# Two stacked attention layers: the stretch between the layers rebuilt, part of the next images' preparation moved into both layers

## The reference

```
layer 0:  f = x Wf + bf   g = x Wg + bg   (8 columns each)   h = x Wh + bh   (64 columns)
          x1 = gamma0 * softmax(g f^T) h + x
layer 1:  q = x1 Wq + bq  k = x1 Wk + bk  v = x1 Wv + bv      (64 columns each)
          out = gamma1 * softmax(q k^T) v + x1
```

## Time and profile before

| what | value |
|---|---|
| median of three runs | 4473.93 us (4473.06 to 4486.53) |
| the profiled execution: time, span | 4475.64 us, 4473.8 us |
| mean granted clock of TensorE | 0.934 |
| busy share: PE, DVE, ACT, POOL | 95%, 74%, 72%, 41% |
| first transposes; first fg_abs; first maxima (L773) | 11.1, 25.76, 86.75 us |
| first scores of layer 0 of image 0; last | 137.8; some 364 us |
| first scores of layer 1 of image 0 | 422.64 us |
| last product of values of layer 1 of image 0 | 671.63 us |

### The profile page before, as it was taken

How to read it: one execution, slowest core, us unless ns; L and a number is a source line. 1 busy time by engine, 2 the same in 40 slices (tenths; PEclk the granted TensorE clock), 3 DMA queues, 4 the chain that set the end, 5 groups by cost and what they waited for, 6 DMA issues and landing times.

```text
span 4473.8 us, 84431 instructions
## 1 busy us (share of the span) xinstructions
PE 4235.0 (95%) x25704; PEld 1535.0 (34%) x25704; DVE 3322.0 (74%) x6409; ACT 3205.1 (72%) x5810; POOL 1826.6 (41%) x845
## 2 busy tenths in 40 slices
PE   5998999989999899999999999999999989999899
PEld 3224332243322533234322433224332243322433
DVE  4776887768777687767877678776887768877687
ACT  1575986659766697657977579775896758967598
POOL 1693008910099001980039600496005940079200
PEclk6897999979999799998999889998999989999799
DMA  0000000000000000000000000000000010000000
GB/s 29 1 11 20 1 1 10 11 20 1 11 1 11 20 1 10 1 11 20 1 11 1 20 10 1 10 1 26 4 1 11 1 29 1 1 11 11 19 1 10
DMA packets 13604, 41.64 MB, mean 9 GB/s; under 512 B 2620, under 2 KB 2620, under 8 KB 10812
## 3 DMA queue, kind: packets, MB, share of 16 engines
q1 hardware_dynamic: 13244, 36.78, 2.7%
HBM read 19.99 MB, written 8.39 MB: 6 GB/s over the span
## 4 chain that ended last, share of the span: by engine, by line
PE 80%; issue 11%; DVE 5%; ACT 3%; POOL 1%; SPq 0%; DVEq 0%; POOLq 0%; DMA 0%; ACTq 0%
PE sum_banks L521 20%; PE score_banks L509 20%; PE sum_banks L430 18%; PE score_banks L410 9%; PE sum_banks L452 3%; PE score_banks L585 3%; PE score_banks L359 2%; PE sum_banks L382 2%; DVE tile_max L773 1%; PE score_banks L344 1%; ACT e_whole L705 1%; POOL e_sum L311 1%; DVE x_abs L882 1%; ACT g_tr L627 1%; ACT f_tr L672 1%
## 5 line engine op out<-in xcount | busy, mean ns | idle before, releaser
L705 ACT ACTIVATE e_whole<-score_banks,exp_bias,down 128x512 f32<-128x512 f32 x2048 | 1574.6, 774 | 215.2 <-DVE o_tr L934 170.4
L311 POOL TENSOR_TENSOR e_sum<-e_sum,e_whole 128x1024 f32<-128x1024 f32 x704 | 1659.5, 2357 | 83.5 <-ACT e_whole L645 32.4
L773 DVE TENSOR_REDUCE tile_max<-sum_banks 128x1 f32<-128x512 f32 (+1 forms) x2128 | 1363.8, 685 | 424.7 <-PE sum_banks L382 421.4
L645 ACT ACTIVATE e_whole<-score_banks,no_bias,down 128x1024 f32<-128x1024 f32 x1024 | 1228.5, 1204 | 546.3 <-PE score_banks L410 536.7
L934 DVE TENSOR_SCALAR_CACHE_REDUCE o_tr<-score_banks,neg_down 128x1024 f32<-128x1024 f32 x1024 | 1314.4, 1284 | 315.7 <-PE score_banks L509 265.9
L430 PE MATMUL sum_banks<-e_whole,proj 128*64 128x512 f32 x4096 | 1119.1, 626 | 0.0
L521 PE MATMUL sum_banks<-e_whole,v_scaled 128*64 128x512 f32 x4096 | 1058.9, 598 | 28.2 <-DVE v_scaled L924 8.4
L308 POOL TENSOR_TENSOR e_sum<-e_whole 128x1024 f32<-128x1024 f32 x32 | 75.5, 2358 | 1930.2 <-ACT e_whole L645 1930.2
L509 PE MATMUL score_banks<-k_high,q_split 128*64 128x512 f16 x4096 | 810.8, 388 | 36.3 <-ACT e_whole L705 18.1
L509 PE MATMUL score_banks<-k_low,q_split 128*64 128x512 f16 x4096 | 803.1, 384 | 0.0
L382 PE MATMUL sum_banks<-f_tr,g_tr 33*128 33x512 f16 x2128 | 695.5, 400 | 21.7 <-DVE tile_max L773 18.6
(11 more groups left out here) (111 smaller groups left out, 2093.9 us busy)
## 6 DMA issues: line engine op xcount, KB each, us to landing
x_in<-in_x_dram SPq DMA_DIRECT2D x19, 1024.0 KB, 4.8
out_dram<-x_mid SPq DMA_DIRECT2D x32, 256.0 KB, 2.7
k_high<-k_high SPq DMA_DIRECT2D x32, 128.0 KB, 2.2
k_low<-k_low SPq DMA_DIRECT2D x32, 128.0 KB, 2.2
gammas<-in_L_conv_gamma_dram SPq DMA_DIRECT2D x2, 0.5 KB
w<-in_L_conv_wg_dram SPq DMA_DIRECT2D x1, 2.0 KB
w<-in_L_conv_bg_dram SPq DMA_DIRECT2D x1, 0.0 KB
w<-in_L_conv_wf_dram SPq DMA_DIRECT2D x1, 2.0 KB
```

Source lines behind the costliest of these rows:

```text
L311: nc.gpsimd.tensor_tensor(acc, acc, e_whole[:, i % U0, :], ALU.add).then_inc(e_added, 1)
L645: nc.scalar.activation(e_whole[:, i % U0, :].rearrange("p (a n) -> p a n", a=2), score_banks[:, 2 * (i % 2):2 * (i % 2) + 2, :], ACT.Exp, ...
L705: nc.scalar.activation(e_whole[:, u, h * BANK:(h + 1) * BANK], score_banks[:, 2 * (u % 2) + h, :], ACT.Exp, bias=exp_bias[:, u:u + 1], sca ...
L773: nc.vector.reduce_max(tile_max[:, blk, j:j + 1], sum_banks[:, (2 + j % banks) % 4, :], AX_X).then_inc(a_used, 1)
```

## The change

The stretch between the layers is made anew, and its parts go to three places.

- **In the stretch** stays the work for layer 1 of this image. The turns of x_mid, the projections of q and k (4 rounds of two banks, one for each half of the partitions) and of V (2 halves) stand between the last four products of values of layer 0. x_tr holds two 64-row halves (pairs of blocks), one array per layer; each product has 64 rows in place of 65, and the biases are added afterwards: q and k by ScalarE (Identity with a bias) and VectorE (scalar_tensor_tensor), V and h by GpSimd (bias_v, bias_h), f and g by VectorE (fg_bias).
- **Into the first seven steps of layer 1** (between_scores) go the last parts of q, k and V and the turns and projections of x of image + 2. VectorE alone copies the turned x_in (turned_x), ScalarE alone empties project0 (projected0, 4 rounds). In the second turn VectorE does fg_bias, fg_scales, fg_scaled and fg_rest; GpSimd does the stacks of both f and g (stack).
- **Into layer 0 of the next image** go the transposes of the stacks, as eight units (turn_unit, turned_unit) in steps 6, 8, ... 20 of chunk 0, and the bound on q and k, now for the image ahead: scans of the turned x in chunk 1 (scan_x), a bound on x_mid in chunk 2 (mid_bound) and on q and k in chunk 3 (qk_bound, qk_power, scales), both from absolute weights and an extra product inside the turn of the chunk before. The scores of the step behind a unit wait for VectorE's copy of it (unit_sb).

The first product of values of a bank starts its sum (start=i == 0) and open_sums goes. The order of queries in a chunk changes (query_col, half_of_chunk). SP issues the second load of x_in after the turns of x of image + 2 and behind the copies of k. There are 25 loads of weights in place of 14. At the start, both images' projections come first; the units of image 1 run in layer 0 of image 0. The core of the diff:

```diff
+        def unit_of(q, i):
+            n, rest = divmod(i - UNIT_AT, 2)
+            return n if q == 0 and rest == 0 and 0 <= n < UNITS else None
...
-                project0(image + 2, par, False)
-                transposes(image, 1, x_mid)
-                for r in range(NCH):
-                    wait_x_tr(pe, image, 1, r)
-                    for k in range(BPC):
-                        t = r * BPC + k
-                        mm = nc.tensor.matmul(score_banks[:, r, k * C:(k + 1) * C], x_tr[:, t * P:(t + 1) * P],
-                                              w1v[:, :], start=True, stop=True)
-                    mm.then_inc(v1_ps, 1)
...
+                pe.wait_ge(a_used, ((image + 1) * NCH + 1) * TILES + EARLY * ATN + FREE_A)
+                pe.wait_ge(x_mid_ready, image * NCH + 2 + FREE)
+                turn_x(1, x_mid, 0, pair_c[:, 0, :])
+                turn_x(1, x_mid, 1, pair_c[:, 1, :])
+                values0(image, par, last, T - 4)
                 pe.wait_ge(exp0_done, (image + 1) * NCH * T + FREE_ST)
                 pe.wait_ge(w1s_ready, image + 1)
+                pe.wait_ge(xt_act, 2 * image + 1)
+                project_qk(par, 0, pair_b)
+                values0(image, par, last, T - 3)
+                pe.wait_ge(x_mid_ready, image * NCH + 3 + FREE)
+                turn_x(1, x_mid, 2, pair_a[:, 0, :])
+                values0(image, par, last, T - 2)
+                pe.wait_ge(xt_dve[1], 2 * image + 1)
+                project_qk(par, 1, pair_c)
+                values0(image, par, last, T - 1)
+                last_sums0(image, last)
+                turn_values0(image, last, pair_d[:, 0, :])
+                pe.wait_ge(xt_act, 2 * image + 2)
+                project_qk(par, 2, pair_a)
+                turn_sums0(image, last, pair_d[:, 1, :])
+                pe.wait_ge(low_done, 2 * (image * NCH + 1))
+                project_v(0, pair_b)
+                pe.wait_ge(x_mid_ready, image * NCH + 4 + FREE)
+                turn_x(1, x_mid, 3, pair_d[:, 0, :])
+
+                def between_scores(u):
+                    if u == 0:
+                        pe.wait_ge(xt_dve[1], 2 * image + 2)
+                        project_qk(par, 3, pair_d)
+                    elif u == 1:
+                        pe.wait_ge(low_done, 2 * (image * NCH + 2))
+                        project_v(1, pair_c)
+                    elif u == 2:
+                        pe.wait_ge(x_loaded, 16 * loads(ahead))
+                        pe.wait_ge(low_done, 2 * (image * NCH + 4))
+                        turn_x(0, x_in, 0, pair_d[:, 0, :])
+                        turn_x(0, x_in, 1, pair_d[:, 1, :])
+                    elif u == 3:
+                        pe.wait_ge(v1_sb, 2 * image + 2)
+                        turn_x(0, x_in, 2, pair_c[:, 0, :])
+                        turn_x(0, x_in, 3, pair_c[:, 1, :])
+                    elif u == 4:
+                        pe.wait_ge(xt_dve[0], ahead * RT + 2)
+                        project0(0, pair_d)
+                    elif u == 5:
+                        pe.wait_ge(xt_dve[0], ahead * RT + 4)
+                        project0(1, pair_c)
+                        pe.wait_ge(pj_act, ahead * RT + 1)
+                        project0(2, pair_d)
+                    elif u == 6:
+                        pe.wait_ge(pj_act, ahead * RT + 2)
+                        project0(3, pair_c)
...
+                turned_x(image, 0, pair_c[:, 0, :])
+                q_high(image, par, 0, pair_b)
+                k_first(image, par, 0, pair_b)
+                turned_x(image, 2, pair_a[:, 0, :])
+                q_high(image, par, 1, pair_c)
                 copy_values0(image, NCH - 1)
...
+                k_first(image, par, 1, pair_c)
+                q_high(image, par, 2, pair_a)
+                k_first(image, par, 2, pair_a)
+                projected_v(image, 0, pair_b)
+                q_high(image, par, 3, pair_d)
+                k_first(image, par, 3, pair_d)
...
+                        if first and u == 0:
+                            q_low(image, par, 3, pair_d)
+                            k_rest(image, par, 3, pair_d)
+                        if first and u in (2, 3):
+                            for r in (2 * u - 4, 2 * u - 3):
+                                turned_x(image + 2, 0, r, (pair_d if u == 2 else pair_c)[:, r % 2, :])
+                        if second and u == 0:
+                            fg_bias(image + 2, par)
+                        if second and u == 4:
+                            fg_scales(image + 2)
+                            fg_scaled(image + 2, par)
+                        if second and u == 7:
+                            fg_rest(image + 2, par)
```

590 lines of the change are left out of this document (343 added, 247 removed).

## The result

The changed kernel took 4299.5 us (median of four runs, 4290.8 to 4307.6) against 4475.4 us for the kernel before: ratio 0.960 (95% interval 0.958 to 0.963), about 4% faster. The forecast was 4277 us; its sum was 22 us too hopeful. The profiled execution has a span of 4293.3 us.

What follows compares the result with a forecast made beforehand. TensorE, busy 95% but partly at a slow clock between the layers, was taken as the bound. Terms summed to -21.8 us per image, -174 for eight, and -22 at the start: 4473.8 to 4277 us, range 4220 to 4330.

Steps and rivals of the forecast that it cites:

- (a): Between layers 0 and 1: with work moved out and woven, layer 1's first scores come at 380.9 against 422.64, -41.7 us.
- (b): First steps of layer 1: projections and turns moved there cost +6.7 us, the scales, fg_high and fg_low on VectorE +2.0.
- (c): Chunk 0 of layer 0: eight units' transposes and VectorE copies delay the next scores, +0.96 each, +7.7 us an image.
- (d): Chunks 1 to 3 of layer 0: four scans, bounds and ten links on VectorE cost about +2.0 us (0 to 4).
- (e): TensorE's clock in 380 to 404, around layer 1's first steps: +1.5 us taken; all at the lower level +9.
- (f): Start of the kernel: first maxima at 64 instead of 86.75, -22.4 us, despite eleven more weight loads.
- R1: Half the gain: clock falls in layer 1's first steps or 64-row halves run separately; either 4320 to 4340 us; chance 0.25.
- R2: Slower: clock falls at chunk 0's first unit and stays down to its end, +31.2 us per image, 4527 us; chance 0.04.
- R4: No change: another wait of 40 us, such as late x_in or k copies, replaces the stretch between layers; chance 0.04.
- R3: Larger gain: units cost +3.7, layer 1's first steps +3, clock nothing; -31 us per image, 4204 us; chance 0.15 with beyond.

## Why the prediction was right, and where its sum was off

The mechanism and the direction were right, and 4299.5 us lies in the range. Point by point:

(a) To the first scores: -41.7 forecast, -41.8 measured in image 0. All its steps stand in the timeline: 15.19 us after the last exp, with VectorE's k_low last. The assumption that the two 64-row halves run together also in fp32 is shown: two products of 512 columns, in four records, take 1.13 us (L416), where the prediction's price for one after the other is 2 x 0.87; eight pairs of the V projection take 2.00 (L408; 1.8 taken).

(b) The first steps: +6.7 and +2.0 forecast, +2.5 and +3.9 measured on average. The first number rests on a misreading: it sets the thirteenth step's exp against the twelfth's of before. Against the thirteenth's (30.0 us) the same schedule gives +4.7, a sum of -23.8 and a forecast of 4261 us, so the misreading brought the forecast nearer by luck. First values 21.7 us after the first scores (23.2 taken). The second number was mis-sized: the prediction left out GpSimd's work in layer 1 as hidden "since GpSimd idles all through layer 1". But VectorE waits there too while GpSimd makes the stacks and adds the biases. L1083, for one, has a median of 163 ns and takes up to 1445 ns there:

```profile
L1083 DVE CUSTOM_DVE_ANT_1 part_scr<-part_sum,chunk_w x256: 160/163/1445, 392.0 to 4280.6; 128x8 f32<-128x8 f32 x128
```

With fg_low, v_scaled and two others such waits make 2.9 us of VectorE an image. How much of the excess of 1.9 us they cause was not tried.

(c) The units: +7.7 forecast; leaving them out gives 7.6 us an image. The step is 2.38 us with TensorE waiting 0.21 for the copy (2.51 forecast). Eight such steps less 1.55 make 6.6, so some 1 us of the 7.6 lies elsewhere and is not traced.

(d) Scans and scales: +2.0 forecast, with a bound of 4, and this is the term that was mis-sized. On average 15.5 us were lost in the four chunks; less (c), that is 7.9. The prediction priced ten links at 0.16 to 0.2 us each, as such links take where GpSimd is idle. Two of them, moved to where GpSimd adds without a pause, take 1.00 and 2.21 us, TensorE stops for 1.82 us and the clock falls. With those two operations in another form 5.3 of the 7.9 us disappear. The cost of an operation was taken from a row where its neighbour was idle and used where it was busy. The remaining 2.6 us is about the forecast of 2.0, and between the exps it lies in chunk 1: there the four scans stand, and there the split of the maxima takes 2.05 us in place of the 0.54 of before and the clock is 0.98 on average instead of 1.00. With the split at 0.72 and the clock at 1.00 (units in the long steps) chunk 1 is 1.1 us shorter.

(e) The clock: +1.5 forecast, nothing measured: 1.00 in all three stages from 365.00 to 410.00 of image 0. What the Trainium skill says in "TensorE: Matmul & The Clock Gate", Part 4, that transposes do not count, is neither borne out nor refuted here: TensorE's turns and products stand mixed in these stages, and no stage of turns alone was measured. The order mattered: with the values issued ahead of the turns it fell to 0.72.

(f) The start: -22.4 forecast, -21.2 measured (first maxima at 65.60, 64.3 forecast). Two misses inside it cancel: the first transpose begins at 20.37 us, 9.3 later and not 5.5, and project0 takes some 3.8 us and not 6.8, since it runs at the upper clock. In the other kernels, whose start is the same but for the clock, the first maxima begin at 64.8 to 68.8.

By image: -0.1 in (a), -2.3 in (b), -0.1 in (c), +5.9 in (d), -1.5 in (e) make +1.9 against the sum of -21.8, which gives the measured -19.9; eight times 1.9 and 1.2 at the start make 16 of the 22 us. The other 6 lie between the span of the changed kernel's profiled execution and the median of its runs, which spread over 17 us.

R1 did not occur: neither the clock nor the halves. R2 did not: the stages of chunk 0's unit steps have 0.98 and 1.00, and chunk 0 grew by 6.9 us. R4 did not: TensorE waits last for VectorE. Of R3 the clock came true and the first steps in part, its cheaper units did not, and (d) took the rest back.
